# Running maxima on GpSimd, and a new order in the gate, expert and last stages of a two-layer transformer kernel

## The reference, cut to what matters

```python
x = x + cross_attention(q=layernorm(x), k=ctx, v=ctx)       # 16 heads of 16, 8 x 512 tokens, D = 256
h = layernorm(x)                                            # ffn: a causal transformer block
r = h + causal_attention(layernorm(h) @ w_qkv) @ w_o
m = layernorm(r)
top_w, top_i = top_k(softmax(m @ w_gate), 2)                # 8 experts, 2 are chosen
x = x + r + sum_e gate_e * (gelu(m @ w1[e] + b1[e]) @ w2[e] + b2[e])
x = x + softmax((layernorm(x)@Wq+bq) @ (ctx@Wk+bk).T) / 16 @ (ctx@Wv+bv)   # one head of 256
x = x + (silu(x @ wg.T) * (x @ wu.T)) @ wd.T                # wg, wu, wd are integers / 127
```

## Time and profile before

| | us |
|---|---|
| median of 3 runs | 2091.76 (2085.29 to 2096.83) |
| profiled execution | 2095.28 |
| its span | 2093.5 |
| PE busy | 1770.4 (85%) |
| DVE busy | 1332.8 (64%) |
| ACT busy | 1098.2 (52%) |
| POOL busy | 570.9 (27%) |

### The profile page before, as it was taken

How to read it: one execution, slowest core, us unless ns; L and a number is a source line. 1 busy time by engine, 2 the same in 40 slices (tenths; PEclk the granted TensorE clock), 3 DMA queues, 4 the chain that set the end, 5 groups by cost and what they waited for, 6 DMA issues and landing times. The chain is left out here.

```text
span 2093.5 us, 40227 instructions
## 1 busy us (share of the span) xinstructions
PE 1770.4 (85%) x13889; PEld 1078.1 (51%) x13890; DVE 1332.8 (64%) x2426; ACT 1098.2 (52%) x2041; POOL 570.9 (27%) x479
## 2 busy tenths in 40 slices
PE   7668888999896889997675599999998469989987
PEld 4312222222673444444564488888887245556555
DVE  6478898996565668883575455555454367767753
ACT  6336777878452567775441244444443246546551
POOL 5244899510430223332366000000000422222000
PEclk9869999999997899998675799999999689999999
DMA  6524665410341121113322211111111411111000
GB/s 186 154 87 140 211 197 179 139 65 2 111 125 60 50 81 49 49 35 130 136 102 82 71 51 45 45 46 50 45 45 41 173 41 51 51 52 50 21 11 21
DMA packets 103208, 171.74 MB, mean 82 GB/s; under 512 B 16008, under 2 KB 78368, under 8 KB 98976
## 3 DMA queue, kind: packets, MB, share of 16 engines
q1 hardware_dynamic: 96928, 153.19, 22.9%
q0 software_dynamic: 6144, 16.79, 2.5%
HBM read 103.34 MB, written 61.87 MB: 79 GB/s over the span
## 5 line engine op out<-in xcount | busy, mean ns | idle before, releaser
L1092 DVE TENSOR_REDUCE a_nm<-a_psS 128x2 f32<-128x1024 f32 (+1 forms) x384 | 446.9, 1191 | 51.4 <-PE a_psS L953 38.3
L1072 ACT ACTIVATE a_prob<-a_psE 128x512 f32<-128x512 f32 (+2 forms) x660 | 335.2, 563 | 122.1 <-PE a_psE L975 120.5
L975 PE MATMUL a_psE<-wall 51*128 51x512 f16 (+3 forms) x1024 | 291.7, 359 | 38.1 <-DMA wall<-a_nrow 26.9
L953 PE MATMUL a_psS<-wall 49*128 49x512 f16 (+4 forms) x1024 | 268.2, 369 | 35.3 <-DVE a_nm L1092 22.6
L1710 ACT ACTIVATE ex_hf<-ex_psH,ex_b 128x256 f32<-128x256 f32 x312 | 130.7, 470 | 216.4 <-PE ex_psH L1741 216.4
L1741 PE MATMUL ex_psH<-ex_xT,wall 128*128 128x256 f16 x1872 | 232.1, 274 | 7.5 <-issue 4.1
L1755 PE MATMUL ex_psY<-wall,ex_hl 128*128 x1872 | 229.8, 273 | 1.4 <-DVEq L1661 0.4
L975 PEld LDWEIGHTS a_psE<-wall 51*128 51x128 f16 x1024 | 76.8, 95 | 276.1 <-ACT a_prob L1072 106.5
L1741 PEld LDWEIGHTS ex_psH<-ex_xT,wall 128*128 x1872 | 182.4, 98 | 34.7 <-issue 13.0
L1755 PEld LDWEIGHTS ex_psY<-wall,ex_hl 128*128 128x128 f16 x1872 | 179.3, 98 | 31.9 <-issue 10.9
L1672 DVE CAST ex_hl<-ex_hf 128x512 f16<-128x512 f32 x156 | 66.6, 427 | 182.2 <-ACT ex_hf L1710 180.4
(11 more groups left out here) (282 smaller groups left out, 3160.0 us busy)
## 6 DMA issues: line engine op xcount, KB each, us to landing
s_qk<-wall SPq DMA_DIRECT2D x32, 512.0 KB, 3.2
wall<-s_qk SPq DMA_DIRECT2D x128, 128.0 KB
xall<-in_w SPq DMA_DIRECT2D x16, 1024.0 KB, 11.8
s_ew<-xall SPq DMA_DIRECT2D x16, 1024.0 KB, 9.2
wall<-s_ew SPq DMA_DIRECT2D x16, 1024.0 KB, 10.6
ex_xt<-s_xs SPq DMA_DIRECT2D x39, 256.0 KB, 2.6
s_ys<-ex_yo SPq DMA_DIRECT2D x39, 256.0 KB, 2.2
t_xin<-in_x SPq DMA_DIRECT2D x16, 512.0 KB, 5.2
```

The source lines that it names most:

```text
L953: last = pe.matmul(psS[:, bank, col:col + n], Q6[s][at:at + SROWS, pr, t * P:(t + 1) * P], K6[s][at:at + SROWS, pr, 0:n], start=True, stop ...
L975: last = pe.matmul(psE[unit % NE][:, col:col + w], K6[s][at:at + EROWS, pr, t * P:(t + 1) * P], Q6[s][at:at + EROWS, pr, S - w:S], start=T ...
L1072: act.activation(prob_of(unit)[:, 0:w], psE[unit % NE][:, 0:w], ACT.Exp, scale=ESC).then_inc(p_ready, 1)
L1092: dve.tensor_reduce(nm[G % NM_BUF][:, t, :, i], psS[:, at:at + 2, 0:n], axis=AX.X, op=ALU.max, negate=True).then_inc(s_free, 1)
```

## The change

In a0 the two VectorE instructions on the maxima become three GpSimd instructions, with a new tile `nscaled`, and GpSimd's program takes turns: the maxima of group i+1, then item i. SP loads a raw item one group sooner. In a1, expert 5 comes in eight pieces of 256 KB at G = 4 to 11. `FIRST_LOADS` becomes 3. In t2, the positions get a place in `psG`, the logits stand before them, the next batch's transposes before the product with the biases, and `weights` before `places` on DVE; the last batch's scatters move into ex, and t2 ends without GpSimd's drain. The tiles of rows for the scatters are now one tile that outlives t2, and ex puts its working tiles over the parts of it that are done. In la, keys and values stand before the combine, and GpSimd's gathers no longer wait for the constants.

```diff
-FIRST_LOADS = 2
+FIRST_LOADS = 3
...
             steps = 0
+            def shift_parts(G):
+                nonlocal steps
+                src = nm[G % NM_BUF][:].rearrange("p t x i -> p (t x) i")
+                dst = nparts[G % 2]
+                pool.wait_ge(s_free, (G + 1) * NPAIR)
+                pool.tensor_scalar(nscaled[:], src, 1.0 / NSC, None, ALU.mult).then_inc(prep_own, 1)
+                steps += 1
+                pool.wait_ge(prep_own, steps)
+                if G >= 2:
+                    pool.wait_ge(nT_ps, G - 1)
+                pool.tensor_copy(dst[:, :, HIGH], nscaled[:]).then_inc(prep_own, 1)
+                steps += 1
+                pool.wait_ge(prep_own, steps)
+                pool.tensor_tensor(dst[:, :, LOW], nscaled[:], dst[:, :, HIGH], ALU.subtract).then_inc(nparts_ready, 1)
+
+            shift_parts(0)
             for i, (src, n, dst, scale, integer) in enumerate(prep):
+                shift_parts(i + 1)
                 raw, pair = raws[i % 2][:, 0:n], prepared[i % 2][:, :, 0:n]
...
+            for G in range(len(prep) + 1, G_ALL):
+                shift_parts(G)
...
                 if not causal:
                     if 2 <= G < len(prep) + 2:
                         pair_store(G - 2)
-                    if 2 <= G < len(prep):
-                        raw_load(G)
-                elif G in (4, 6):
-                    k = (G - 4) // 2
-                    sp.dma_start(scr["ew_to"][:, 5, k], scr["ew"][5, k]).then_inc(scr["ew_in"], 16)
+                    if 2 <= G + 1 < len(prep):
+                        raw_load(G + 1)
+                elif 4 <= G < 12:
+                    k, half, part = (G - 4) // 4, (G - 4) // 2 % 2, slice((G - 4) % 2 * 1024, (G - 4) % 2 * 1024 + 1024)
+                    sp.dma_start(scr["ew_to"][:, 5, k, half, part], scr["ew"][5, k, :, half, part]
+                                 ).then_inc(scr["ew_in"], 16)
...
-                    if p < 2 and G + 1 < G_ALL:
+                    if causal and p < 2 and G + 1 < G_ALL:
                         shift(G + 1, p)
...
-    with nc.Block() as block:
+    with nc.Block(no_gpsimd_drain=True) as block:
...
-                if has(k - 1):
+                if has(k - 1) and k < B:
                     scatter(k - 1, (0, 1))
...
+            for t in range(TT):
+                scatter_rows(pool, scr["xs"], slots, B - 1, t, last_rows, xs_out[(B - 1) % 4])
...
-            pool.wait_ge(const_in, 16 * n_const)
...
             context_low(0, 0)
+            keys_low(0, 0)
+            values(0)
+            values_low(0, 0)
+            context_low(1, 1)
             combine(0, 0, 0)
             combine(0, 0, 1)
             stats_of(xin[0])
             att_norm(0, 0)
             att_norm_low(0)
-            context_low(1, 1)
-            keys_low(0, 0)
-            values(0)
-            values_low(0, 0)
```

More of the change, by code:

```diff
@@ L907, in _ @@
                     shift_rows(G + 1)
[L908 to L912, removed]
+                if G < len(late):
+                    heads.load(sp, *late[G], qk, mask)
                 if G >= 2 and G // 2 + SLOTS - 1 < NHB:
@@ L1124, in _ @@
                     top(G, p)
-                    if G == 1 and p < 2:
+                    if causal and G == 1 and p < 2:
                         shift(0, p)
@@ L1135, in _, with scatter_rows, phase_gates @@
             normalise(G_ALL - 1)
-def phase_gates(nc, c, w, scr, oall, xall, norm1, ew_to, ew_in, slots, gsel, hist, ones, xs_out):
-    y = [c.sb(f"y{p}", [P, TT, D]) for p in range(4)]
+def scatter_rows(pool, xs, slots, n, t, rows, out):
+    for k in range(CHOSEN):
+        at = n * TT + t
+        pool.indirect_dma_start(xs, bass.IndirectOffsetOnAxis(slots[:, k, at:at + 1], 0), rows[:, t, :], None
+                                ).then_inc(out, 16)
+def phase_gates(nc, c, w, scr, oall, xall, norm1, ew_to, ew_in, slots, gsel, hist, ones, xs_out, y):
     xres, oT = ([c.sb(f"{n}{p}", [P, TT, D]) for p in range(2)] for n in ("xres", "oT"))
@@ L1238, in scatter @@
                 for t in tiles:
[L1239 to L1242, removed]
+                    scatter_rows(pool, scr["xs"], slots, n, t, y[n % 4], xs_out[n % 4])
             for k in STEPS:
@@ L1358, in _ @@
                 if has(k):
+                    weights(k)
                     places(k)
-                    weights(k)
                     chosen_gates(k)
@@ L1465, in _ @@
                     transposes(pe, psU, oall[:, n], ident[:]).then_inc(u_ps, 1)
+                n = k + 1
+                if has(n):
+                    pe.wait_ge(z_ready, n + 1)
+                    if n >= 1:
+                        pe.wait_ge(yT_ready, n)
+                    transposes(pe, psT, y[n % 4], ident[:]).then_inc(tr_ps, 1)
                 n = k - 1
@@ L1476, in _ @@
                 if has(n):
[L1477 to L1483, removed]
                     pe.wait_ge(yT_ready, n + 1)
                     if n >= 1:
-                        pe.wait_ge(slot_ready, n)
+                        pe.wait_ge(l_free, n)
                     for t in range(TT):
@@ L1491, in _, with phase_experts @@
                     last.then_inc(l_ps, 1)
-def phase_experts(nc, c, scr, ew_to, ew_in, slots, hist, ones, xs_out):
-    xt = [c.sb(f"xt{p}", [P, 2, D]) for p in range(2)]
-    xf = [c.sb(f"xf{p}", [P, DC, TE]) for p in range(2)]
-    hf = c.sb("hf", [P, FC, TE])
+                if has(k):
+                    positions(k)
+def phase_experts(nc, c, scr, ew_to, ew_in, slots, hist, ones, xs_out, ys_tile, last_rows):
+    moving = Arena(ys_tile)
+    xt = [moving.take([P, 2, D]) for p in range(2)]
+    xf = [moving.take([P, DC, TE]) for p in range(2)]
+    hf = moving.take([P, FC, TE])
     hl = [c.sb(f"hl{p}", [P, 2, FC, TE], F16) for p in range(2)]
@@ L2276, in _ @@
             context_high(0, 0)
+            keys_high(0, 0)
+            context_high(1, 1)
+            values_high(0, 0)
             att_norm_high(0)
[L2278 to L2280 removed]
             att_transposed(0)
```

24 lines of the change are left out of this document (12 added, 12 removed).

## The result

The changed kernel takes 2197.1 us (median of 4 runs, 2194.8 to 2200.4) against 2094.0 for the kernel before (median of 4): a ratio of 1.0501, interval 1.0465 to 1.0537. It is 5% slower, as forecast (2177, range 2100 to 2230). The profiled execution's span is 2192.7 us against 2093.5, and the table says where the 99 us come from. A stage runs from its first instruction to the first of the next.

What follows compares the result with a forecast made beforehand. VectorE was taken to bound a0. 2095.3 + 131 (a0) + 1 (t0, t1) - 15 (a1) - 28.5 (t2, ex) - 3.7 (la) = 2180; the profiled execution being 3.5 above the median, 2177 us, range 2100 to 2230.

Steps and rivals of the forecast that it cites:

- The loop: In a0, each group's maxima hang on a store that the maxima before released: 21.4 us a group, 20.2 to 25.
- Rival A: In a0, the raw load binds instead of the store: 15.0 us a group, 2069 us in all; chance 0.07.
- B: In a0, GpSimd runs at its own pace of 12.4 us, no transfer in the way: 2026 us; chance 0.05.
- One sign: In a0's profile after, GpSimd's CAST waits 5 to 9 us for the store, once in each of groups 2 to 21.
- The six small items: In a0, items 16 to 21 take 16 us each, 13 to 18: together 96 against 73.3 before, so +23.
- the last groups: In a0, the ten groups after GpSimd is done with items take 10.6 us each and together return 9 us.
- Rival C: In a0, the store is alone and lands in half of its 9.2 us: loop 16.8, about 2104 us; chance 0.10.
- the new order of t2: In t2, logits start 2.7 us earlier and positions no longer wait: 2.2 in six rounds, -13 us, bounds 0 and -25.
- the drain goes: Between t2 and ex, the drain of 6.1 us goes, so ex begins within 2 us of t2's last scatter.
- the new order at -3.7: In la, values, transposes and copies leave the path behind the combine, which is delayed 1.6: -3.7 us, bounds 0 and -6.
- the bound of -18: In a1, quarter-size weight pieces and early heads take nearly all of TensorE's 13.5 us of row waits: -15, between -10 and -18.
- t0 and t1: In t0 and t1, the third block's issues move ahead of a stage's end: 1.0 us charged for both, bounds 0 to 2.9 a stage.

Runs made afterwards that it cites:

- The first run: Changed kernel with SP issuing the store of item G-2 ahead of the rows of group G+1 in a0: 2058.9 us, ratio 0.985.
- the second one: Changed kernel with the store of item G-2 and the raw load of item G+1 both ahead of the rows in SP's step: 2023.1 us, ratio 0.967.

## Why the prediction was right, and where it was not

**The loop was the step that decided, and it held.** Each of its terms is in the changed trace: maxima 0.83 (taken 0.85), to the rows 1.36 (1.15), rows to store 4.24 (4.24), store 9.3 (9.2), CAST and subtraction 6.0 (6.1), in sum 21.7 against 21.4. Fourteen loops took 303.8 us (167.22 to 471.03) where 299.6 were forecast. The first run, in which one issue moves and 138 us return, shows the cause rather than argues it. Rival A, the raw load as the next limit, was no outcome of the change, but it is what that run meets, and B's 12.4 is what the second one meets. (A's terms add up to 2067.6, not to 2069.) One sign was off: the CAST waits 9.4 us on average, not 5 to 9; the forecast's own terms give 9.2 for it (1.15 + 4.24 + 9.2 - 5.37).

**That the sum came within 1% is in part luck.** a0 cost 19 us more than forecast and t2 with ex gained 9 less; la, which gained 9 more, and a1, which gained 4 more, hid about half of that.

**a0 was 19 us too low in size.** The six small items took 17.4 each (471.03 to 575.64), not 16: +8.6. The loops gave +4.2, their start 0.6. The rest is the last groups, for which I had given 9 us back and of which 6 did not come: I had said that VectorE bounds a group when GpSimd rests. Four such groups in the kernel before, then four in the changed one (the windows' columns as above):

```profile
455.00:498.30 43.30, 41.72 (x291) 11.04 (x288) 40.91 (x49) 37.60 (x73) 0.00 (x0) 1.00 0.05 14
```

```profile
588.00:631.30 43.30, 41.46 (x290) 11.04 (x291) 40.40 (x41) 37.27 (x73) 2.71 (x12) 1.00 0.15 48
```

TensorE is busy for over 41 of 43 us in both, at a granted clock of 1.00, and waits for no maxima. With 0.3 us of work less a group on DVE the rows still go out 10.8 us apart: TensorE and DVE had stood side by side, and DVE alone was not the bound that the prediction made it.

**The rule of the Trainium skill weighed there** ("DMA: Bandwidth & Descriptors", section "Anatomy of one DMA — SWDGE (gpsimd) path") would have put the store at 4.4 us and the loop at 16.6, both estimates. That section fits transfers which GpSimd issues, and SP issues this store, so the trace does not contradict the page; it shows that the fit can't be taken over here. The store, issued beside a load and heads, takes 9.1 in the median, and the loop is 21.7. Rival C falls with it.

**t2 and ex gained 20, not 28.5.** DVE's end came 150.0 us into the stage instead of 162.8, -12.8, as much as was forecast for the new order of t2 (-13); no run undoes that order alone, and in the run with the maxima on VectorE this end came at 145.9, so it scatters by some 4 us. The further 3 us on the way to that end did not come, and the step that failed is "the drain goes": I read the flag on the block and not the meeting behind it. That is 4.6 us, and the runs with semaphores alone show it. ex, which now has the last scatters, came out 2.3 us longer (taken 0.4).

**la: the right sign, the wrong step.** I had priced the new order at -3.7. The order costs 3.3, and the 6.4 that came (at TensorE's 320th matmul, the old order with early gathers against the kernel before) are from GpSimd's removed wait, which I had listed among the diff's parts and given no term. DVE's combine had waited 12.3 us for the gathers, in a row for which I had not asked what lets the gathers start. The first score came 44.9 us into the stage instead of 47.6, not 4 us earlier. The further 10 us of la have no term in the prediction either, and their cause stays open: about 6 of it is a pause in the kernel before,

```profile
DVE la_top L2066 <- issue: 7.8, 1, 7.8
```

which the traces of the changed kernel and of all four variants that I compared lack, the one with the old order too. The trace shows two transfers on the queue that it calls `q14 instruction` within that pause; that DVE waited for them is not shown. Some 4 are at the end, where TensorE's granted clock was 0.93 in the kernel before (its last 45.9 us) and 1.00 in the changed one (the last 42.2, the same instructions). These 10 us can hardly all be an accident of the one execution that was traced: its 2095.3 us lie only 1 to 4 above the medians of the kernel before. So whether the change has a part in them the runs do not settle.

**a1** came to -19 for -15, just past the bound of -18. Where I named the pieces first, the runs show the heads first.

**t0 and t1** came to +0.7 for +1, by luck. a0 begins 6.5 us after VectorE's last instruction of t0 (111.10 to 117.61), where it was 3.8 (113.40 to 117.18): the third block's issues now stand there. They were hidden by an earlier end of VectorE's work, which the change does not explain. Of the variants, the two with two blocks have t0 at 114.7 and 114.9 us, the ten with three at 118.5 to 121.6, so by these the block costs some 3 to 5 us there (an estimate) rather than 1.

## What to carry to other kernels

Before a small step is moved to an engine with room, follow what already stands in that engine's queue: the price here was not 0.7 us of work but a wait for a store which an earlier result of the same step released, and that made a circle. Such a circle shows when one asks of each wait "what must have been issued, and behind what does that stand", and it can be cut by moving one issue. When one limit goes, look for others of the same height before pricing the gain; and a wait taken from a queue deserves a term as much as an added one does.

## What was not expected of the hardware

GpSimd's drain behind its indirect transfers takes 4.6 us here even when the last of them was issued 2 us earlier and had landed, and leaving it out of one place moved it to the next that had one. Small operations on GpSimd are cheap here (0.25, 0.20 and 0.23 us on 128x16), while VectorE's scaling of the same shape had taken 2.28 us beside GpSimd's long one.
